# Preparing each chunk of a selective scan one chunk sooner, and storing its step rows first

## What is computed

```python
u = silu(conv(u)); dt, Bm, Cm = split(x_dbl)
dt = softplus(dt @ dt_proj_w.T + dt_proj_b)
def step(h, inputs):
    dA = exp(dt_t[:, :, None] * A)
    h = dA * h + (dt_t * u_t)[:, :, None] * B_t[:, None, :]
    y = einsum('bdn,bn->bd', h, C_t)
y = (ys + u * D) * silu(z)
```

## Time and profile before

| | us |
|---|---|
| median of 3 runs (1936.26 to 1938.16) | 1937.62 |
| the profiled execution, its own time | 1938.45 |
| span of its trace, first to last instruction | 1936.7 |
| scans of layer 0, first one to last read-out | 70.08 to 576.19 |
| scans of layer 1, first one to last read-out | 1092.57 to 1600.26 |

### The profile page before, as it was taken

One profiled execution on the slowest core, in us unless ns is written; L12 is line 12 of the kernel. 1 busy time (PEld: TensorE's weight loads), 2 busy tenths in 40 slices (PEclk: granted clock), 3 DMA queues, 4 the chain that ended last, 5 costly groups with the idle time before them and its releaser, 6 DMA issues. The chain is left out here.

```text
span 1936.7 us, 25492 instructions
## 1 busy us (share of the span) xinstructions
PE 1546.9 (80%) x6220; PEld 927.2 (48%) x6221; DVE 1271.6 (66%) x2146; ACT 991.2 (51%) x1594; POOL 1211.5 (63%) x1179
## 2 busy tenths in 40 slices
PE   5677777777778998999982687777777777699996
PEld 3222222222228998989981222222222227566664
DVE  5799999999996531111115799999999996411012
ACT  4777777777772211222223777777777772122112
POOL 2699999999981001444435699999999992123310
PEclk8799999999995899999995799999999995599997
DMA  5788777787774204777765877788877881423313
GB/s 131 191 183 185 181 179 177 176 186 179 178 160 155 85 25 143 233 220 218 226 162 134 206 179 176 179 182 179 181 176 174 184 186 49 171 78 122 123 62 107
DMA packets 104507, 311.06 MB, mean 161 GB/s; under 512 B 19389, under 2 KB 74509, under 8 KB 93069
## 3 DMA queue, kind: packets, MB, share of 16 engines
q1 hardware_dynamic: 91896, 291.72, 60.1%
q0 software_dynamic: 12544, 18.63, 4.1%
HBM read 258.83 MB, written 51.45 MB: 160 GB/s over the span
## 5 line engine op out<-in xcount | busy, mean ns | idle before, releaser
L689 POOL TENSOR_TENSOR mamba_dbu<-mamba_rep 128x462 f32<-128x462 f32 x640 | 677.2, 1085 | 66.1 <-DMA mamba_rep<-dt_rows 66.1
L509 PE MATMUL mamba_ysum<-mamba_hc,all_sel 128*128 128x462 f32 x800 | 379.4, 588 | 148.3 <-DVE mamba_hc L797 147.3
L621 ACT ACTIVATE mamba_state<-mamba_rep,all_m_acol 128x462 f32<-128x462 f32 x640 | 388.9, 638 | 156.6 <-DVE mamba_last L808 155.6
L811 DVE TENSOR_TENSOR_SCAN mamba_state<-mamba_state,mamba_carry,mamba_dbu 128x462 f32<-128x462 f32 x400 | 455.4, 1179 | 0.0
L509 PEld LDWEIGHTS mamba_ysum<-mamba_hc,all_sel 128*128 128x128 f32 x800 | 130.3, 190 | 398.3 <-DVE mamba_hc L797 318.8
L808 DVE TENSOR_TENSOR_SCAN mamba_last<-mamba_state,mamba_last,mamba_dbu 128x462 f32<-128x462 f32 x240 | 280.3, 1168 | 15.2 <-POOL mamba_dbu L689 12.4
L684 POOL TENSOR_TENSOR mamba_hcp<-mamba_last,mamba_rep 128x462 f32<-128x462 f32 x240 | 266.7, 1111 | 5.6 <-DVE mamba_last L808 5.6
L504 PE MATMUL mamba_ysum<-mamba_hcp,all_sel 128*128 128x462 f32 x480 | 227.8, 570 | 50.1 <-POOL mamba_hcp L684 50.0
L797 DVE TENSOR_TENSOR mamba_hc<-mamba_state,mamba_rep 128x462 f32<-128x462 f32 (+1 forms) x240 | 230.7, 961 | 0.0
L1433 DVE TENSOR_TENSOR moe_h<-moe_sg,moe_up 128x512 f32<-128x512 f32 x62 | 42.6, 688 | 283.0 <-PE moe_up L1242 276.6
L504 PEld LDWEIGHTS mamba_ysum<-mamba_hcp,all_sel 128*128 128x128 f32 x480 | 85.3, 190 | 172.4 <-POOL mamba_hcp L684 119.6
(11 more groups left out here) (236 smaller groups left out, 2285.6 us busy)
## 6 DMA issues: line engine op xcount, KB each, us to landing
mamba_rep<-bc_rows SPq DMA_DIRECT2D x168, 462.0 KB, 7.4
mamba_rep<-dt_rows SPq DMA_DIRECT2D x168, 462.0 KB, 7.5
weights_wgu<-in_L_gu_dram SPq DMA_DIRECT2D x88, 512.0 KB
dt_rows<-mamba_dd SPq DMA_DIRECT2D x168, 115.5 KB, 7.2
weights_w<-in_L_w_dram SPq DMA_DIRECT2D x16, 1024.0 KB
mamba_xs<-seq_scratch SPq DMA_DIRECT2D x92, 116.0 KB, 9.2
seq_scratch<-mamba_y SPq DMA_DIRECT2D x40, 116.2 KB, 7.0
normed_rows<-xn SPq DMA_DIRECT2D x16, 288.0 KB, 7.1
```

Of the source, the lines that this page charges most:

```text
L509: nc.tensor.matmul(ysum[:, 0:TC], sel[:, i // NM, :], hc[:, n % HCD, :], start=False, stop=end).then_inc(hc_summed, 1)
L621: nc.scalar.activation(state[:, STATE_BANK[i], 0:TC], rep[:, par * REP_ROWS + i // NM, :], ACT.Exp, scale=m["acol"][:, i:i + 1]).then_inc( ...
L689: pool.tensor_tensor(dbu[:, i % 4, :], rep[:, first + NG + i // NM, :], rep[:, first + 2 * NG + i % NM, :], ALU.mult).then_inc(dbu_ready, 1)
L811: nc.vector.tensor_tensor_scan(bank, bank, dbu[:, i % 4, :], carry[:, i:i + 1], ALU.mult, ALU.add).then_inc(scan_done, 1)
```

## The change

- Preparation of a chunk made sooner: PE makes u and z of chunk k+3 inside chunk k (`AT_U` = 10, behind the eleventh matmul of the sum), and `prep_dt`, `prep_bc` of chunk k+2 at the start of chunk k; those of chunk 2 are made ahead of the loop. `prep_silu` moves from item 6 to 2, `prep_exp` 10 to 6, `prep_one` 11 to 7, `prep_bc` 13 to 8, `prep_ln` 15 to 10; on DVE `prep_rr` from 13 to 9, and its `prep_ln` and `prep_dt` from behind item 15 to behind scans 11 and 12.
- POOL's step product moves from behind item 3 to behind item 1 of the next chunk.
- SP's turn begins with `store_dt(k+1)`, ahead of the waits for chunk k-1; `store_bc` comes ahead of `load_xs`, which now is that of chunk k+4. `dt_rows` has two halves, `seq_scratch` one more chunk, filled by one more DMA in layer 0, and `load_xs(3)` comes ahead of the loop.
- `gate` moves from behind scan 2 to behind scan 3.

```diff
-AT_SILU, AT_EXP, AT_ONE, AT_LN, AT_BC, AT_DT, AT_DTU, AT_Y, AT_RR = 6, 10, 11, 15, 13, 3, 3, 2, 13
+AT_SILU, AT_EXP, AT_ONE, AT_BC, AT_LN, AT_U, AT_DTU, AT_Y, AT_RR, AT_LR, AT_ADD = 2, 6, 7, 8, 10, 10, 1, 3, 9, 11, 12
...
             def store_dt(k):
                 sp.wait_ge(front_pool, START + k + 1)
+                half_rows = g["dt_rows"][bass.ds(half(k), 1), :, :]
...
             sp.wait_ge(seq_rest, 16 * RESTS)
+            sp.wait_ge(front_mm, START + MMS * 2 + MM_Z)
+            load_xs(3)
             tiles["room_free"](sp)
             with sp.Fori(0, NCH) as k:
...
+                store_dt(k + 1)
                 sp.wait_ge(decay_ready, items_before)
                 sp.wait_ge(dbu_ready, items_before)
                 sp.wait_ge(hc_ready, START + ND * k)
                 sp.wait_ge(hcp_ready, START + NP_ * k)
                 sp.wait_ge(rep_loaded, replicas_before)
                 replicate_bc(k + 1)
-                store_dt(k + 1)
                 replicate_dt(k + 1)
-                sp.wait_ge(front_mm, START + MMS * (k + 2) + MM_Z)
-                load_xs(k + 3)
                 store_bc(k + 2)
+                sp.wait_ge(front_mm, START + MMS * (k + 3) + MM_Z)
+                load_xs(k + 4)
...
+            prep_u(2)
+            prep_z(2)
             with pe.Fori(0, NCH) as k:
-                prep_u(k + 2)
-                prep_z(k + 2)
-
+                prep_dt(k + 2)
+                prep_bc(k + 2)
                 pe.wait_ge(y_ready, START + k)
...
-                    if at == AT_DT:
-                        prep_dt(k + 2)
-                    if at == AT_DT + 1:
-                        prep_bc(k + 2)
+                    if at == AT_U:
+                        prep_u(k + 3)
+                        prep_z(k + 3)
...
                         if i == AT_RR:
                             prep_rr(k + 2)
+                        if i == AT_LR:
+                            prep_ln(k + 2)
+                        if i == AT_ADD:
+                            prep_dt(k + 2)
...
-                    prep_ln(k + 2)
                     read_out(ITEMS - 2 if SECOND[ITEMS - 1] else ITEMS - 1)
-                    prep_dt(k + 2)
```

More of the change, by code:

```diff
@@ L307, in phase_mamba @@
         LAG = 2 * GT - 1
-        RESTS = NCH - 3 + (3 if l == 0 else 0)
+        RESTS = NCH - 3 + (4 if l == 0 else 0)
         AT_W, AT_U0, AT_DT0, AT_U1, AT_DT1, AT_RR0, AT_DTU0 = ((7, 11, 14, 18, 20, 5, 19), (99, 11, 14, 18, 20, 5, 19))[l]
@@ L341, in store_dt @@
                 sp.wait_ge(front_pool, START + k + 1)
+                half_rows = g["dt_rows"][bass.ds(half(k), 1), :, :]
                 for q in range(NG):
-                    rows = g["dt_rows"].rearrange("(d w q) n -> q d w n", w=2, q=NG)[q]
+                    rows = half_rows.rearrange("o (d w q) n -> q (o d) w n", w=2, q=NG)[q]
                     sp.dma_start(rows, dd[q * DG:(q + 1) * DG, :, :]).then_inc(dt_stored, 16)
@@ L355, in replicate_dt @@
                 row = rep_row(k)
-                src = g["dt_rows"].rearrange("(d w) n -> d (w n)", d=DG)
+                src = g["dt_rows"][bass.ds(half(k), 1), :, :].rearrange("o (d w) n -> (o d) (w n)", d=DG)
                 sp.wait_ge(dt_stored, 16 * NG * (k + 1))
@@ L372, in _ @@
                 sp.wait_ge(zeroed, 1)
-                for k in range(NCH, NCH + 3):
+                for k in range(NCH, NCH + 4):
                     sp.dma_start(g["seq"][k], hc[0:DM, :, :].rearrange("p n c -> p (n c)")[:, 0:CW]).then_inc(seq_rest, 16)
@@ L417, in _ @@
                 replicate_bc(k + 1)
-                store_dt(k + 1)
                 replicate_dt(k + 1)
-                sp.wait_ge(front_mm, START + MMS * (k + 2) + MM_Z)
-                load_xs(k + 3)
                 store_bc(k + 2)
+                sp.wait_ge(front_mm, START + MMS * (k + 3) + MM_Z)
+                load_xs(k + 4)
             sp.wait_ge(rep_loaded, 16 * REPS * (NCH + 1))
             sp.wait_ge(bc_stored, 16 * (NCH + 2))
-            sp.wait_ge(xs_loaded, 32 * (NCH + 3))
+            sp.wait_ge(xs_loaded, 32 * (NCH + 4))
+            sp.wait_ge(dt_stored, 16 * NG * (NCH + 1))
             if l == 0:
@@ L1740, in build @@
                 ("wout", [P, DM]), ("vec", [P, 3]), ("diag", [P, DI]), ("acol", [P, ITEMS]))})
-        g["seq"] = nc.dram_tensor("seq_scratch", (NCH + 3, DM, CW), F32, kind="Internal").ap()
-        g["dt_rows"] = nc.dram_tensor("dt_rows", (2 * P, TC), F32, kind="Internal").ap()
+        g["seq"] = nc.dram_tensor("seq_scratch", (NCH + 4, DM, CW), F32, kind="Internal").ap()
+        g["dt_rows"] = nc.dram_tensor("dt_rows", (2, 2 * P, TC), F32, kind="Internal").ap()
         g["bc_rows"] = nc.dram_tensor("bc_rows", (2, 2 * DS, TC), F32, kind="Internal").ap()
```

## The result

The changed kernel takes 2014.4 us (median of 4 runs, 2008.9 to 2018.3), the one before 1937.9 (4 runs): a ratio of 1.039, interval 1.037 to 1.042. It is 76.5 us slower, where 15 us less were forecast.

A forecast was written before the change was run, and what follows sets the result against it. A chain through POOL's step product, store and replication was taken to hold chunks above DVE's 24.91 us. Removing DVE's waits gains 17.2 us, less 2.2 for thin places: 1937.62 - 15 = 1922.6 us, range 1919.5 to 1931.

The forecast's parts named there:

- X: Time from SP's store of the step rows to the replicas' landing; forecast 20.5 us, bounds 20.0 and 21.8, formerly 20.1.
- T: Moment in a chunk when the replicas have landed and POOL goes on; needed 2.9 us ahead of scan 0.
- half rule: With a longer X, DVE stalls by half the excess over 21.2 us, since a stall also delays the next chunk.
- So the chain closes on itself: Replicas, POOL's step product, SP's store and replication sum to 25.46 us, the distance of two T, setting the period.
- the new chain: After the change: step product 3.25 us after POOL's start, then store leading all replication, 4.26 MB, until T.
- The gap: DMA stretch ahead of `replicate_dt`, 410.85 to 412.85 at share 0.22; claimed to go with the store first.
- The chain as the bound: Rival: the DMA chain still sets the period, X up to 22.1 us, time 1932 to 1937.6 us; chance 0.17.
- The silu block as a rival: Rival: ACT's silu block, waiting for PE's u and z, delays exponential 3 and scan 3; 1959 us, chance 0.10.
- The tail on table loads: Rival: each ACT table switch in the silu block costs 1.4 us more; 1961 us, chance 0.02.
- The gate free: Moving the gate behind scan 3 costs nothing, as PE's sum of the chunk before is done by then.
- DVE's unstalled 24.91: A chunk takes 24.91 us when DVE never waits; DVE's changed order of operations adds no cost.
- Scan 2 behind the step product: POOL's product for scan 2 now follows the step product; a thin place of 0.36 us, within 2.2 us allowed.

The follow-up runs named there:

- before_store_first: The kernel before with the store of the step rows first in SyncE's turn and two halves of `dt_rows`; 2082.9 us in a single run.
- after_product_item3: The changed kernel with POOL's step product back behind item 3; 2076.9 us in a single run.
- before_split: The kernel before with the B and C replication split, two DMAs each side of the step rows' store; 1919.0 us, ratio 0.990.
- after_split: The changed kernel with the B and C replication split around the step rows' store and `load_xs(k+3)` away from the turn's end; 1952.3 us, ratio 1.008.

## Why the prediction was wrong

**What the change does to SyncE's queue.** The step that failed is "X, from store to T, is then 20.5 us (bounds 20.0 ..., 21.8 ...)". It measures 23.8 in the changed kernel and 23.9 in `before_store_first`. It comes to 23.9 on average over layer 0 of the changed kernel. Its terms in the chunk shown, from the windows above: until the replication's data flow it takes 4.0 us at 134 GB/s (the four stores are issued over 3.06 us instead of 2.57, and 0.77 more pass to the next issue), where the prediction's terms allow 3.3 (4.0 us at 134 GB/s are 0.54 MB, 2.5 us at 217, and 0.42 + 0.4 on top). Then 18.3 us at 211 GB/s, where 20.5 - 3.3 = 17.2 were left; the rate was lower than 217, and the windows hold some 0.2 MB more than the 4.26 counted, from the DMAs beside. And 1.5 us from 420.75 to the replicas, which had no term at all: the DMA share is 0.21 there, and nothing is transferred in the last half microsecond. In the kernel before `load_xs` and `store_bc` transferred in that time, so that the windows showed busy DMA engines up to T, and this last wait could not be seen.

**The time that follows from X.** With 23.8 for X the prediction's own terms for the loop, 3.25 + X, give 27.05 us a chunk, and the trace has 27.35. But the prediction turned a longer X into time by its half rule: 24.91 + (23.8 - 21.2)/2 = 26.2 us a chunk, some 1970 us. So the size of X failed first, and the half rule hid what such an X would cost.

**The chain of the kernel before.** "So the chain closes on itself" was a sum of segments that fit, and no proof: segments from one T to the next always add up to the distance of the two. The store's 8.75 us were mostly a wait in the queue, and an earlier product did not shorten them (1943 us). The end of the preceding chunk released `replicate_bc`, and 23.7 us from there led to T. With the store first, the product and the whole 4.26 MB do stand in line. The prediction had the new chain right in its members (`before_store_first` and `after_product_item3`, which test them, came within 2 and 9 us of the differences expected), but took its start to be where the old one was, and counted as a gain of 2.07 us what had been slack.

**The gap.** That the 2 us without transfers ahead of `replicate_dt` would go was right, and worth what it promised: `before_split` all but closes it alone and meets the 24.91 us bound. The price was named too, that nothing is transferred between T and the store; with X at 20.5 it seemed to fit under DVE's time.

**The rivals.** The chain as the bound was the true one; it was given 0.17, capped at 22.1 us, and its formula shared each stall with the next chunk. That is true while POOL waits for scans; once it waits for replicas, all of the excess falls on the period. So no case reached 2014. The silu block as a rival was right in kind: with the queue as it was, 27 us of DVE's waits are for exponentials, for a T that was to come 2.9 ahead of scan 0 and came 2.1 ahead in the chunk read (409.99 for 412.05). The tail on table loads did not show: from 427.81 to 431.51 in `after_split` the block of two loads and two silus is 3.70 us again.

**Smaller steps.** The gate free: shown. DVE's unstalled 24.91: shown by `before_split` for the old order; the changed order, called free, takes 25.08. Scan 2 behind the step product: 28.2 us of waits in the changed kernel, far over the allowance, since T came late. The wait of SyncE on PE's z at the end of a turn had no term; it cost a little in some chunks here, and some 14 us once `replicate_bc` stood behind it.

## What to carry to other kernels

A chain whose segments add up to the period is not yet the chain that sets it. Of every segment that holds a DMA, ask whether it waits for its issue or behind others in the queue; moving the issue alone tells. A long transfer that needs nothing new belongs ahead of a short one that does, and splitting it around the short one fills both the wait for the producer and the landing. The landing of the last transfer is a term of its own, even where other transfers hide it in the DMA share.

## What the hardware showed

The same four stores took 2.57 us to issue with fixed DRAM addresses and 3.06 with addresses from a register (3.04 in `before_store_first`), and landed 2.4 us after issue with nothing long ahead of them, 7.2 behind 1.9 MB. In the changed kernel the DMA share was 0.00 from 421.75 on, and POOL's first product started at 422.25: the waiting engines go on half a microsecond or more after the last transfer.

TensorE's granted clock was 0.52 over 415.45 to 421.45 of the changed kernel, its lower level of 1.2 GHz for nearly the whole window, where it was 1.00 in the chunk read before the change. Ahead of it PE stood for 2.67 us:

```profile
416.49 3.45 PE L514 MATMUL mamba_ysum<-mamba_hc,all_sel 128*128 128x462 f32 x4 [2.67 <-DVE mamba_hc L801]
419.73 1.75 PE L450 MATMUL mamba_front<-mamba_xs,all_m_wu 128*128 128x462 f32 x2
```

The clock was still 1.00 at 415.0 to 415.5, in the gap, and 0.50 at 416.0 to 416.5, before the gap ended. The u product took 1.75 us behind it, and 1.01 in the next chunk, at 445.51, behind a gap of 2.53 us in which the clock stayed at 1.00. What decides between the two is open.
